# A transformer block with a routed expert layer on one core: the last normalisation steps rebuilt as one list of parts, returns issued without fills, transfers moved to other tiles

## What is computed

```python
x = layernorm(x + causal_attention(x, W_Q, W_K, W_V))
logits = (x @ gate_w + gate_b) / 0.9
gate_probs = softmax(where(top2(logits), logits, -inf))
h = gelu(einsum('bsd,edf->bsef', x, w1) + b1)          # E = 8, F = 512
expert_out = einsum('bsef,efd->bsed', h, w2) + b2
out = einsum('bse,bsed->bsd', gate_probs, expert_out)
out = (out - mean) / sqrt(var + 1e-5) * ln_g + ln_b     # first norm of the end
return layernorm(x + out)                               # second norm of the end
```

## Time and profile before

| what | value |
| --- | --- |
| median of 3 runs | 287.6 us (287.13 to 287.66) |
| the profiled execution | 285.26 us |
| its span, first to last instruction | 283.5 us |
| granted TensorE clock, mean | 0.940 |
| PE busy | 235.7 us (83%) |
| PEld busy | 213.9 us (75%) |
| DVE busy | 171.8 us (61%) |
| ACT busy | 181.3 us (64%) |
| POOL busy | 178.6 us (63%) |

### The profile page before, as it was taken

How to read it: one execution, slowest core, us unless ns; L and a number is a source line. 1 busy time by engine, 2 the same in 40 slices (tenths; PEclk the granted TensorE clock), 3 DMA queues, 4 the chain that set the end, 5 groups by cost and what they waited for, 6 DMA issues and landing times.

```text
span 283.5 us, 7517 instructions
## 1 busy us (share of the span) xinstructions
PE 235.7 (83%) x1867; PEld 213.9 (75%) x1868; DVE 171.8 (61%) x947; ACT 181.3 (64%) x537; POOL 178.6 (63%) x296
## 2 busy tenths in 40 slices
PE   2898998999997697999999999999967999992000
PEld 2566876878876486999989999999957999992000
DVE  0047577788888764459532333565247759976984
ACT  3265848777756378888874655555534589778733
POOL 8200028488888888888888888888887565657000
PEclk9999999999999759999999999999999999998555
DMA  4999102212212525332338778674189797331722
GB/s 121 273 327 283 42 2 84 68 49 75 85 49 83 143 58 144 77 79 65 94 85 260 230 266 270 177 225 129 46 275 339 270 275 253 145 107 46 224 81 75
DMA packets 44802, 42.38 MB, mean 149 GB/s; under 512 B 5440, under 2 KB 33520, under 8 KB 44768
## 3 DMA queue, kind: packets, MB, share of 16 engines
q1 hardware_dynamic: 40448, 33.10, 39.9%
q0 software_dynamic: 4320, 8.92, 9.1%
HBM read 27.89 MB, written 12.01 MB: 141 GB/s over the span
## 4 chain that ended last, share of the span: by engine, by line
POOL 32%; PE 30%; issue 10%; ACT 9%; DVE 8%; DMA 5%; SPq 3%; DVEq 1%; ACTq 1%; POOLq 0%
POOL returned L1294 15%; POOL slots L1287 11%; PE bank L555 8%; PE bank L544 8%; POOL pause_out L1280 6%; PE bank L409 3%; ACT pair L695 3%; DMA slot_x<-slots 2%; PE bank L395 2%; PE bank L436 2%; PE bank L457 2%; ACT h L690 2%; PE bank L400 1%; PE bank L476 1%; DMA slots<-rows,slot_of 1%
## 5 line engine op out<-in xcount | busy, mean ns | idle before, releaser
L690 ACT ACTIVATE h<-bank,b_cols 128x128 f32<-128x128 f32 x284 | 81.2, 370 | 48.9 <-PE bank L544 48.1
L1294 POOL DMA_INDIRECT returned<-x,slot_back x71 | 75.0, 1057 | 30.2 <-POOL pause_out L1280 18.6
L555 PE MATMUL bank<-w_all,h 128*128 x568 | 78.7, 282 | 0.0
L544 PE MATMUL bank<-slot_xT,w_now 128*128 128x128 f32 x568 | 77.1, 280 | 0.9 <-issue 0.9
L1287 POOL DMA_INDIRECT slots<-rows,slot_of x64 | 62.1, 970 | 17.8 <-POOL pause_out L1280 17.5
L544 PEld LDWEIGHTS bank<-slot_xT,w_now 128*128 128x128 f32 x568 | 71.3, 197 | 1.1 <-issue 1.1
L555 PEld LDWEIGHTS bank<-w_all,h 128*128 128x128 f32 x568 | 69.0, 192 | 1.0
L1280 POOL MEMSET pause_out<- 1x200 f32 x131 | 33.4, 255 | 34.2 <-DVE rows L912 34.0
L818 DVE CAST slot_back<-slot_x 128x1 uint32<-128x1 f32 x71 | 10.7, 151 | 53.2 <-PE bank L544 52.9
L777 DVE TENSOR_REDUCE negmax<-bank 128x1 f32<-128x128 f32 (+3 forms) x32 | 14.7, 485 | 19.4 <-PE bank L410 19.1
L476 PE MATMUL bank<-ident,slot_x 128*128 128x128 f32 x71 | 20.6, 291 | 6.0 <-DMA slot_x<-slots 6.0
(11 more groups left out here) (160 smaller groups left out, 313.1 us busy)
## 6 DMA issues: line engine op xcount, KB each, us to landing
w_now<-in_L_ffn_w_dram SPq DMA_DIRECT2D x47, 256.0 KB, 4.0
slot_x<-slots SPq DMA_DIRECT2D x71, 65.0 KB, 2.8
w_all<-in_L_ffn_w_dram SPq DMA_DIRECT2D x16, 256.0 KB, 5.6
pair<-returned SPq DMA_DIRECT2D x16, 256.0 KB, 3.8
x<-n_L_attn_embeddings_dram SPq DMA_DIRECT2D x8, 256.0 KB, 4.1
rows<-rows SPq DMA_DIRECT2D x8, 256.0 KB, 2.7
returned<-x,slot_back POOLq DMA_INDIRECT x71, 2.7
slots<-rows,slot_of POOLq DMA_INDIRECT x64
```

Of the source, the lines that this page charges most:

```text
L544: m = nc.tensor.matmul(o, w1_now[:, s, cols], slot_xT[:, s % RING, :], start=True, stop=True)
L555: m = nc.tensor.matmul(o, h[:, s % RING, c * P:(c + 1) * P], w2_c, start=False, stop=(c == FC - 1))
L690: m = nc.scalar.activation(h[:, s % RING, cols], bank_[:, cols], ACT.Gelu, bias=b1_cols[:, c:][:, bass.ds(first, 1)])
L1294: g_.indirect_dma_start(returned, bass.IndirectOffsetOnAxis(ap=slot_back[:, j:j + 1], axis=0), y[:, j % Y_RING, :], None).then_inc(y_retur ...
```

## The change

- DVE and ACT: `final_units`, `set_rstd` and the two-units-a-tile rule go. One list FINAL holds the parts of batches 0 to 5, each with a cost; from tile 48 (FINAL_AT) `finished_by(j)` hands out 5.3 cost units to a tile. The first norms of batches 0, 1, 4, 5, 6 and 7 are the fused form; those of 2 and 3 go over ACT (tiles 58 to 61).
- All roots of the end are taken on ACT. Two of them stand inside the tile loop, after the gelus of tiles 55 and 68 (ROOT_AT), seven behind it. The second norm of batches 0 to 3 moves behind the loop.
- POOL: `give_back` has no pause any more; the dispatches keep theirs.
- SP: the pair loads of batches 0 to 3 move from tiles 53 to 56 to tiles 55 to 58. The eight padding writes (fill_pads) move from one block before tile 24 to one per tile at tiles 16 to 23, behind a new wait (`pads_known`). copy_rows(6) and copy_rows(7) each move behind some slot loads, and the slot loads 4 and 5 get a wait for the last attention copies.
- DVE: the parts of rest_table are packed to end with tile 13 rather than 15.

```diff
-        LOAD_AT = {b: WHOLE[0] + 14 + b for b in range(4)} | {b: WHOLE[1] + 10 + b for b in (4, 5)}
+        LOAD_AT = {b: WHOLE[0] + 16 + b for b in range(4)} | {b: WHOLE[1] + 10 + b for b in (4, 5)}
-        HEAD_AT, TAIL_AT, UNITS_A_TILE = 49, 59, 2
-        NORM_AT = ((0, 57), (1, 69))
+        FINAL_AT, FINAL_SHARE = WHOLE[0] + 9, 5.3
+        NORM_FROM, NORM_AT, ROOT_AT = 2 * TB, 58, (55, 68)
-        ROOTS = ((4, 6), (6, 7), (4, 5), (5, 6), (7, 8), (7, 8), (6, 7))
+        ROOTS = ((0, 4), (0, 5), (5, 6), (4, 5), (5, 6), (6, 7), (6, 7), (7, 8), (7, 8))
...
+                sp.wait_ge(pads_known, 1)
...
                 if s == AHEAD + 1:
+                    sp.wait_ge(pT_ready, (B - 1) * UNITS + 1)
+                elif s == AHEAD + 2:
+                    sp.wait_ge(pT_ready, B * UNITS)
+                elif s == AHEAD + 3:
                     copy_rows(B - 2)
                 load_slots(s, at)
-            copy_rows(B - 1)
...
                     load_slots(s, at[s])
+                    if i == PADS_IN:
+                        fill_pads(s, pads[s])
+                    if j == UNROLL + AHEAD - 1:
+                        copy_rows(B - 1)
...
-            for e, at in enumerate(pad_rows()):
-                fill_pads(e, at)
...
+                        if j in ROOT_AT:
+                            take_root(ROOT_AT.index(j))
+                        if j == NORM_AT:
+                            act.wait_ge(scaled, 1)
+                        t = NORM_FROM + 2 * (j - NORM_AT)
+                        if NORM_FROM <= t < EARLY:
+                            normalise(t, normed)
...
-            nc.scalar.activation(unused[:], ones[:, 0:1], ACT.Sqrt)
...
+            HEAD = [("add", 3), ("stats", 4), ("aggregate", 2)]
+            FUSED = [("centre", 5), ("rescale", 5), ("stats", 4), ("aggregate", 2)]
+            PLAIN = [("scale", 3), ("plus", 3), ("stats", 4), ("aggregate", 2)]
+            FINAL = [(what, b, cost) for b in range(4) for what, cost in HEAD]
+            FINAL += [("centre", 0, 5), ("centre", 1, 5), ("root", 0, 3)]
+            FINAL += [(what, b, cost) for b in (0, 1) for what, cost in FUSED[1:]]
+            FINAL += [(what, b, cost) for b in (2, 3) for what, cost in PLAIN]
+            FINAL += [(what, b, cost) for b in (4, 5) for what, cost in HEAD]
+            FINAL += [("centre", 4, 5), ("root", 1, 3)]
+            FINAL += [(what, 4, cost) for what, cost in FUSED[1:]]
+            FINAL += [("centre", 5, 5)]
...
             def give_back(j):
-                if j < J - 4:
-                    pause(NT * TOPK + j + 1 if j >= RETURNS_AHEAD else NT * TOPK - TB * TOPK + j + 1)
                 pool.wait_ge(y_ready, j + 1)
```

More of the change, by code:

```diff
@@ L206, in moe_block @@
         dispatch_ready, numbers_ready = sem("dispatch_ready"), sem("numbers_ready")
+        pads_known = sem("pads_known")
         dispatched = [sem(f"dispatched{g}") for g in range(2)]
@@ L696, in scale_and_shift, with normalise @@
                                             bias=sum_shift[:, k:k + 1], scale=sum_rstd[:, k:k + 1])
-            def normalise(second, first, end):
-                act.wait_ge(moments_ready, second + 1)
-                for t in range(first, end, 2):
-                    scale_and_shift(t)
-                    scale_and_shift(t + 1).then_inc(res_ready if second else normed, 1)
+            def normalise(t, done):
+                scale_and_shift(t)
+                scale_and_shift(t + 1).then_inc(done, 1)
             def take_root(r):
@@ L1284, in dispatch @@
                 for k in range(TOPK):
-                    pause((b * TB + t) * TOPK + k + 1 + (RETURNS_AHEAD if b == B - 1 else 0))
+                    pause((b * TB + t) * TOPK + k + 1)
                     c = k * TB + t
```

175 lines of the change are left out of this document (73 added, 102 removed).

## The result

The changed kernel takes 279.9 us (median of 4 runs, 277.0 to 281.9) where the kernel before took 287.4 on the same chip; the ratio is 0.968 (0.961 to 0.976). On a second occasion it took 278.6 us against 286.5: ratio 0.975 (0.971 to 0.979). So the change makes the kernel faster by 7 to 9 us. The forecast was a gain of 6.9 us and a time of 280.7, with 279.2 as the low end of the range.

The account below looks back on a forecast made before the run. PE bounds tiles 4 to 70 at 2.006 us a step, leaving two holes and the end to win. Terms -5.5 + 0 + 0 - 1.4 = -6.9 us gave a span of 276.6 and a time of 280.7 us, range 279.2 to 284.5.

Parts of the forecast that it names:

- The hole at tiles 54 to 58: PE's stop behind tile 53: returns without pauses and pair loads two tiles later remove it whole, -5.5 us.
- SP's longest wait on returns under 2 us: Sign on SP's timeline that would show the forecast right; the wait before was read as 12.6 us.
- Dispatches and tables: POOL's last dispatch and the moved rest_table: between 0.7 us earlier and 0.5 us later, taken as 0.
- Padding: SP's new wait for pads_known ahead of tiles 16 to 23: cost 0, with 2.3 us of cover.
- Roots between the gelus: ACT's two roots inside the tile loop, 2.9 us each with table loads: cost 0, covers 0.8 and 0.6 us.
- DVE in the loop: DVE's bodies 48 to 70 sum to 41.5 us against PE's 46: cost 0.
- The end: DVE's work behind the last weighing: -1.4 us, bounds 0 to -2.
- a shift (0.25): New DVE work counted in the end's sum, 0.25 us beside 4.4 us of fused halves.
- returns follow each other in 1.26 us and not in 1.50: Rival on POOL: pauses cost nothing, returns keep 1.5 us; 284.2 us, chance 0.08.
- the idle time at the end: Rival: the end gains nothing, idle time becomes another wait between ACT and DVE; 282.1 us, chance 0.13.
- table switch reached PE: Rival on ACT: each load between gelus costs as much again, +3.8 us; 284.5 us, chance 0.06.
- nothing was slower: Rival on POOL: back-to-back returns collide each time at a pitch of 2.0 us; +6.6 us, 294 us, chance 0.05.

Follow-up runs that it names:

- the longer run: First profile of the changed kernel, with no further edit; span 280.0 us.
- the shorter run: Second, later profile of the same changed kernel, taken in e5; span 275.2 us.
- e2: Kernel before with only the pauses ahead of the returns taken away; 280.5 us, ratio 0.977 to the kernel before.
- e8: Changed kernel with the pair loads of batches 0 to 3 back at tiles 53 to 56; 278.0 us, ratio 0.971 to the kernel before.
- e1: Kernel before with only the pair loads of batches 0 to 3 moved two tiles later; 282.6 us, ratio 0.985 to the kernel before.
- e6: Changed kernel with the parts of rest_table handed out as before; 279.1 us, ratio 0.976 to the kernel before.
- e9: Changed kernel with an extra unused gelu and root on ACT behind the root at tile 55; 281.8 us, ratio 0.984 to the kernel before.
- e3: Changed kernel with the pauses ahead of the returns and the old pair-load tiles put back; 284.0 us, ratio 0.989 to the kernel before.
- e11: Kernel before with all pauses gone, on dispatches and returns; 275.9 us, ratio 0.968 to the kernel before.
- e10: Changed kernel without pauses before the dispatches either, a repeat of e4; 273.9 us, ratio 0.958 to the kernel before.
- e4: Changed kernel with the pauses ahead of the 64 dispatches taken away as well; 274.7 us, ratio 0.956 to the kernel before.
- e12: Changed kernel without any pause and with FINAL_SHARE 5.5 in place of 5.3; 272.9 us, ratio 0.954 to the kernel before.
- e5: Changed kernel once more, unedited, beside the kernel before; 278.6 us, ratio 0.975.

## Why the prediction was right or wrong

**The hole at tiles 54 to 58, -5.5 us: right.** It closed by 5.5 us (ladder, tile 53 to 58), by the steps that were written down: returns 1.26 us apart (POOL, the longer run, from the last dispatch on), POOL caught up with y (at return 35 in the shorter run; forecast was 36), pair loads at 197, tile 56 at 200.3.

```profile
147.19 0.96 POOL L1280 DMA_INDIRECT slots<-rows,slot_of  x1 [0.28 <-POOL pause_out L1273]
148.46 0.96 POOL L1285 DMA_INDIRECT returned<-x,slot_back  x1 [0.31 <-DVE x L1053]
149.73 0.96 POOL L1285 DMA_INDIRECT returned<-x,slot_back  x1 [0.30 <-issue]
```

What it didn't say is that the missing pauses are enough by themselves (e2, e8), and that the later loads are, too, for a PE that comes 2.7 us late (e1). Its own cover of 7 us was the hint: with so much to spare, one of two edits may do nothing. It also took the 12.6 us of the earlier trace rows for the wait at tile 53, which is 11.4, and so its sign "SP's longest wait on returns under 2 us" didn't come (11.7, ahead of the pair load of batch 7); no sum used either. The collisions with ln_b's adds cost 0.2 us each (1.15 in place of 0.96), not 0.5, and nothing, since POOL waits for y there.

**Dispatches and tables, 0: the first term that was mis-sized.** The text weighed 0.7 us from three missing pauses against a change of collisions, and took 0 from bounds of -0.7 and +0.5. Measured from the ninth to the last dispatch: 88.77 and 88.95 us in the old code, 88.27 on the mean of four profiles in the new (87.87 to 88.79), so -0.6; in the pair of profiles compared above it is -0.9 on POOL and -0.8 at tile 25, while the longer run has the same as before. The pauses and the collisions can be told apart. In every one of these profiles two transfers of POOL are stretched beyond 0.96 us, and their excess is 1.8 and 2.1 us in the old code and 1.7 to 2.7 in the new. Without it 86.8 to 87.0 us are left with pauses and 86.1 to 86.3 without: that is the 0.7. What the collisions take is another matter; e2 is the old code with only the pauses ahead of the returns gone, and its second and third return take

```profile
129.50 2.34 POOL L1292 DMA_INDIRECT returned<-x,slot_back  x1 [0.31 <-DVE x L1044]
132.15 2.40 POOL L1292 DMA_INDIRECT returned<-x,slot_back  x1 [0.30 <-DVE x L1044]
```

where before has 1.54 and 2.17; so e2 needs 88.94 us and gained nothing there. The table in its new place costs about what it does in the old (e6). So 0.7 should have been booked, and the collisions left in the range, with a little over 1 us between the mildest and the worst. The rule that tile 25 follows the last dispatch one for one held: it is transposed 4.4 to 4.6 us behind it wherever it waited less than 2.2 us. Where it waited longer (e9, e1, e3) it comes 5.0 to 5.3 us behind it, and why stays open.

**Padding, 0: right.** In the shorter run SP waits 7.7 us for `pads_known`, tile 16 is loaded at 122.01, just before the first fill at 122.52 (the prediction had 123.5 for the tile), and PE's steps from tile 9 to 24 are 2.0 us each. e11 against e10 shows that the old block of fills cost nothing either.

**Roots between the gelus, 0: right, with a cover of 1.6 us in place of 0.8.** In the shorter run gelu 56 is done at 221.18 + 1.14 = 222.32 and expansion 59 starts at 223.93:

```profile
218.26 1.28 ACT L713 ACT_TABLE_LOAD   x1
219.55 0.31 ACT L713 ACTIVATE sum_var<-sum_moments,eps 128x16 f32<-128x16 f32 x1
219.88 1.28 ACT L696 ACT_TABLE_LOAD   x1
221.18 1.14 ACT L696 ACTIVATE h<-bank,b_cols 128x128 f32<-128x128 f32 x4
...
223.93 1.06 PE L550 MATMUL bank<-slot_xT,w_now 128*128 128x128 f32 x8
```

The 1.1 us that were set aside for the registers of the next tiles don't show in ACT's row, where the table load starts 0.02 us behind the root. The Trainium skill (ScalarE: Activation LUTs, What ACT_TABLE_LOAD costs) adds a drain of about 1380 ns to each load; by the rows of e9 there is none in this kernel, also not behind gelus, which the trace of before could not show. An estimate from that page's figure, two drains less the cover of 1.6 us, would have made PE wait by 1.2 us for the single root, and no run shows that.

**DVE in the loop, 0: right.** From 202 to 249 us of the shorter run PE is busy for 47.00 of 47 us, DVE for 39.5.

**The end, -1.4: the second term that was mis-sized; measured -2.05.** It is the same in every kernel with the new end (36.3 to 36.4 us behind tile 70) against every one with the old (38.4). From the last weighing to the end it is 24.0 us in the shorter run, where the prediction had 24.7. The idle 2.01 us did go, and the parts that were listed as gone and as new are those of the two timelines. The step that failed is "and a shift (0.25)", that is, the price of the roots. DVE's roots in the shorter run:

```profile
257.61 0.38 DVE L1076 BATCH_NORM_AGGREGATE sum_moments<-sum_stats 128x2 f32<-128x6 f32 x4
257.91 0.14 DVE L1091 RECIPROCAL sum_rstd<-sum_var 128x4 f32<-128x4 f32 x1
258.13 0.16 DVE L1061 SCALAR_TENSOR_TENSOR sum_shift<-sum_moments,sum_rstd 128x4 f32<-128x4 f32 x1
258.21 0.68 DVE L1068 TENSOR_TENSOR pair<-pair 128x512 f32<-128x512 f32 x1
```

This one costs 0.30 us from its reciprocal to the start of the next work; another costs 0.51 (266.50 to 266.81 is a second cheap one, 267.86 to 268.37 a dear one). The kernels' source tells the two kinds apart: behind a dear one stands a dve.drain(), and the next work starts 0.25 or 0.26 us behind the start of the shift; in a cheap one, whose next work (here the add for batch 6) doesn't read the root, there is none, and it starts 0.08 us behind it. In the new order three of the seven roots behind the last weighing have no drain behind them; before, all seven had one, and they took 0.50 to 0.54 us, but for one of 0.26 that had no shift. Summed, the seven take 2.96 us against 3.35, where I had added 0.25: that is 0.6 of the 0.65 us. The rest of the sum has errors of 0.1 to 0.25 us that cancel. No run moves a drain alone, so this is read from rows and source, not tested.

**The sum and its level.** For the two profiles of like start the terms should have read -5.5 - 0.8 - 2.05 = -8.35, and they differ by 8.3; forecast was -6.9. So the step that failed is the size of two terms: the dispatches were put at 0 where 0.6 to 0.8 us were gained, and the roots of the end at +0.25 where they gave back 0.39. Which instructions go and which come was told rightly in both. Both errors went the same way, each to the far end of its bounds, and the range reached no further than those two ends together from a median that itself moves by up to 1.5 us from one chip to the next (287.6, 286.65, 286.5, 286.1). It also had no term for the run's own spread: the ninth dispatch alone comes at 55.7 to 58.6 us, and the ratio of the first occasion is known to 2 us, not to the 0.6 that the prediction took. On which side of 279.2 one measurement falls is in part luck.

**The rivals.** All fell: without pauses the returns follow each other in 1.26 us and not in 1.50, and the hole closed; no wait took the place of the idle time at the end; no table switch reached PE until it was doubled (e9); and POOL's pitch stayed at 1.26 us, so that nothing was slower.

## What to carry to other kernels

When two edits aim at one hole, work out what each closes alone; a cover of several microseconds behind the pair says that one of them may be idle. An engine with a queue of its own (here POOL) can make losses exchangeable: what the engine that waits for it (here PE) loses early it doesn't lose late, so single edits don't add up until the queue has slack, and then they do (e10 against e11). And compare profiles by a ladder of like instructions, with like starts, before dividing a difference into causes.

## What the runs showed of the hardware

In all fourteen profiles TensorE's granted clock is at or near the lower level in a part of 96 to 112 us (0.50 to 0.57 in at least one stretch of 4 us), where attention ends and PE is busy for a part of the time only. Beyond that it falls in some profiles and not in others, for reasons that the traces don't settle. In attention, four of fourteen (e4, e6, e12, the longer one of the changed kernel) have 0.91 in 40 to 60 us, and their ninth dispatch comes at 58.0 to 58.6 us in place of 55.7 to 56.8. In 112 to 116 us e4, e8 and e12 have 0.63 to 0.73. Behind tile 25 the step to tile 26 takes 3.7 to 3.8 us in the longer run, e1 and e3, after waits of 1.85, 3.46 and 3.32 us, and in e9, after a wait of 2.53 us, the two steps behind it take 2.85 and 3.00; it takes 2.2 in e5 after a wait of 2.13 us. What decides between them stays open.

A transfer of POOL that runs beside one of DVE's two 1.68 us instructions takes up to 2.40 us in place of 0.96 (2.47 in e11). The places change with the start, and so does the sum: the two excesses together are 1.65 us in e3 and 2.82 in e2. Removing pauses didn't make two transfers of POOL slow each other: 71 returns of the changed kernel have a mean of 1.035 us, and 57 of the 63 steps from one dispatch of e10 to the next are 1.26 or 1.27 us.
